# A third buffer for a block's scores and transpositions one slot later, in the attention stage of a decoder layer

## The reference, cut to what matters

```python
x = x + mamba_block(layernorm(x))                       # state-space block
x = x + cross_attention(ctx, ctx, layernorm(x), mask)   # 16 heads of 32, 750 keys
x = x + ffn(layernorm(x))                               # 512 -> 2048 -> 512, binarized weights
```

```python
qh = split_heads(q @ Wq + bq); kh = split_heads(k @ Wk + bk); vh = split_heads(v @ Wv + bv)
logits = einsum('bhqd,bhkd->bhqk', qh, kh) / sqrt(32) + mask * -1e9
attn = softmax(logits, axis=-1)
out = einsum('bhqk,bhkd->bhqd', attn, vh).merge_heads() @ Wo + bo
```

## Time and profile before

| | |
|---|---|
| median of three runs | 3586.39 us |
| the profiled execution | 3583.32 us, span 3582.0 us |
| PE busy over the span | 3233.6 us (90%) |
| DVE, ACT, POOL busy | 2664.0, 2390.2, 1804.9 us (74%, 67%, 50%) |
| exponentials, L1290 | 512 of 914 ns |
| mask and minimum, L1404 | 1024 of 544 ns |
| transpositions, L1163 | 3072 of 290 ns |
| copies of tiles 0 and 2, L1299 | 512 of 536 ns |

### The profile page before, as it was taken

The page is one execution under the profiler, slowest core; times in us unless marked ns, Lnnn a source line. Parts: engine busy times, 40 slices in busy tenths (PEclk is TensorE's granted clock), DMA queues, the critical chain, the costliest instruction groups (busy, mean ns, idle before and its releaser), DMA issues. The chain is left out here.

```text
span 3582.0 us, 59831 instructions
## 1 busy us (share of the span) xinstructions
PE 3233.6 (90%) x20864; PEld 2270.0 (63%) x20864; DVE 2664.0 (74%) x4673; ACT 2390.2 (67%) x5339; POOL 1804.9 (50%) x1211
## 2 busy tenths in 40 slices
PE   5699989898898988988997998999999999899999
PEld 4566655666566655666554666666666666678887
DVE  2899999999999999999984776667676676622222
ACT  5777888778877788777863667666666666622222
POOL 2678887888878888888873000000000000045454
PEclk8899999999999999999999999999999999999999
DMA  5576766667666766676564041111211121111010
GB/s 163 153 187 189 190 173 158 179 178 192 174 158 180 190 171 162 173 196 180 159 166 158 4 122 61 46 46 60 75 47 46 51 79 54 30 57 43 24 48 24
DMA packets 286282, 425.03 MB, mean 119 GB/s; under 512 B 28737, under 2 KB 226113, under 8 KB 281378
## 3 DMA queue, kind: packets, MB, share of 16 engines
q1 hardware_dynamic: 278621, 411.44, 41.1%
q10 hardware_dynamic: 7365, 9.77, 0.9%
HBM read 320.12 MB, written 101.02 MB: 118 GB/s over the span
## 5 line engine op out<-in xcount | busy, mean ns | idle before, releaser
L810 POOL TENSOR_TENSOR a_hs<-a_rep,a_bmat 128x896 f32<-128x896 f32 x512 | 1061.8, 2098 | 287.7 <-PE a_yps L322 286.3
L442 ACT ACTIVATE a_states<-a_rep,a_a_neg 128x224 f32<-128x224 f32 x2048 | 793.5, 437 | 90.2 <-DVE a_hs L706 88.2
L699 DVE TENSOR_TENSOR_SCAN a_states<-a_states,a_hs 128x900 f32<-128x900 f32 x384 | 779.8, 2031 | 75.6 <-ACT a_states L442 60.9
L1404 DVE CUSTOM_DVE_ANT_0 b_sc<-sps,early_mask 112x375 f32<-112x375 f32 x1024 | 499.8, 544 | 155.6 <-PE sps L1147 155.5
L1163 PEld LDWEIGHTS b_tps<-ident,b_sc 112*125 112x125 f32 x3072 | 404.1, 192 | 287.1 <-issue 167.9
L1163 PE MATMUL b_tps<-ident,b_sc 112*125 112x112 f32 x3072 | 493.6, 290 | 77.6 <-DVE b_pT L1418 36.4
L1290 ACT ACTIVATE b_sc<-b_sc,b_nmax 112x750 f32<-112x750 f32 x512 | 467.3, 914 | 62.9 <-DVE b_nmax L1410 62.7
L1546 POOL TENSOR_SCALAR b_x_var<-mv 112x2 f32<-112x2 f32 x16 | 3.4, 213 | 898.5 <-DVE mv L1455 898.5
L344 PE MATMUL a_work<-early_scan_hT,w_in 128*128 128x224 f32 x2048 | 425.6, 363 | 10.4 <-issue 7.5
L344 PEld LDWEIGHTS a_work<-early_scan_hT,w_in 128*128 128x128 f32 x2048 | 396.7, 196 | 51.5 <-issue 44.3
L706 DVE TENSOR_TENSOR a_hs<-a_states,a_cmat 128x896 f32<-128x896 f32 x384 | 419.0, 1091 | 13.2
(11 more groups left out here) (199 smaller groups left out, 5017.8 us busy)
## 6 DMA issues: line engine op xcount, KB each, us to landing
a_rep<-du_scratch SPq DMA_DIRECT2D x512, 224.0 KB, 5.7
w_in<-W_in_dram SPq DMA_DIRECT2D x128, 512.0 KB, 4.3
du_scratch<-early_du SPq DMA_DIRECT2D x16, 1792.0 KB, 11.6
ctx<-ctxT_dram SPq DMA_DIRECT2D x48, 500.0 KB, 5.9
v_scratch<-kv_out SPq DMA_DIRECT2D x96, 250.0 KB
k_scratch<-kv_out SPq DMA_DIRECT2D x96, 250.0 KB, 4.5
b_keys<-k_scratch SPq DMA_DIRECT2D x8, 1500.0 KB, 9.5
b_v<-v_scratch SPq DMA_DIRECT2D x8, 1500.0 KB
```

Of the source, the lines that this page charges most:

```text
L442: e = act.activation(rows(states[:, g % DA, :])[:, q, 1:ROW], rep[tile % REPS][:, j, 0, :], ACT.Exp, scale=a_neg[:, g % SLOTS, q:q + 1])
L699: dve.tensor_tensor_scan(state if g % G4 else whole, state, whole, 0.0, ALU.mult, ALU.add).then_inc(S["scan"], 1)
L810: pool.tensor_tensor(hs[g % RING][:, :, 1:ROW], rep[tile % REPS][:, j, 1, :].unsqueeze(1).broadcast_to([P, Q, L]), bmat[b % 2][:], ALU.mul ...
L1404: dve.tensor_tensor_reduce(out=sc[block % 2][:, j, cols], in0=sps[0:TT, j, 0:HALF], in1=mask[:, block % 2, cols], scale=-1.0, scalar=3.0e3 ...
```

## The change

Scores get a third buffer, `sc2`, which lies in the region `shared`. There it takes the place of the first half of w1, so this half is loaded near the end of the stage only: block n uses buffer n mod 3 up to block 122, and from block 123 on (`THREE`) two buffers in turn. The load of the first half of w1 waits for all transpositions of the first 123 blocks and stands at slot 249; its two signs stand in ACT's slots 254 and 255. The other half is loaded at slot 32 as before, with its two signs in slots 48 and 49. `nmax` has three places instead of two.

Transpositions and their copies move one slot later (`slot - 3`), for all tiles. Weighing the values, spreading the sums and keeping them (`rb`) move from slots 2, 6, 10, 14 to 3, 7, 11, 15, and `scale_o` from 3, 7, 11, 15 to 4, 8, 12, 0. Inverting the sums stays in slots 2, 6, 10, 14. The second output projection and its residual move from slot 7 to slot 6. At the end of the stage, the rows of the feed-forward part are normalised and transposed a little earlier.

```diff
         stats = mem.sbuf("stats", [TT, 2, 6])
-        sc = [mem.sbuf(f"sc{i}", [TT, GROUP, KEYS]) for i in range(2)]
+        sc = [*(mem.sbuf(f"sc{i}", [TT, GROUP, KEYS]) for i in range(2)),
+              mem.inside("sc2", [TT, GROUP, KEYS], shared.scores)]
         half_min = mem.sbuf("half_min", [TT, 2, GROUP])
-        nmax = mem.sbuf("nmax", [TT, 2, GROUP])
...
         LAST = (B - 1) * SLOTS
-        ROWS_AT = (LAST + 13, LAST + 15, LAST + 16, LAST + 17)
+        ROWS_AT = (LAST + 12, LAST + 13, LAST + 16, LAST + 17)
+        THREE = LAST // 2 + 3
+        assert THREE % 3 == 0 and (GROUP * KEYS <= 2 * F)
         tps = mem.psum("tps", [P, 2, BANK])
         ups = mem.psum("ups", [P, 2, BANK])
...
 
         slots = range(-6, B * SLOTS + SLOTS // 2 + 4)
         unit_of, bank_of = {}, {}
+
+        def buffer_of(block):
+
+            return block % 3 if block < THREE else (block - THREE) % 2
+
+        def used_by(block):
+
...
                 if 0 <= slot < N_ALL:
                     scores(slot)
                 if before:
-                    transpose_p(slot - 2, 0)
+                    transpose_p(slot - 3, 0)
                 for b in range(B):
                     at = slot - b * SLOTS
                     if -3 <= at < -3 + SLOTS and (at + 3) % 4 == 0:
                         project_q(b, (at + 3) // 4)
-                    if 6 <= at < 6 + SLOTS and (at - 6) % 4 == 0:
-                        weigh_v(b, (at - 6) // 4)
+                    if 7 <= at < 7 + SLOTS and (at - 7) % 4 == 0:
+                        weigh_v(b, (at - 7) // 4)
                 if before:
-                    transpose_p(slot - 2, 1)
+                    transpose_p(slot - 3, 1)
                 for b in range(B):
                     at = slot - b * SLOTS
                     if at == -4 and b:
                         transpose_h(b, 0)
                         transpose_h(b, 1)
-                    if 6 <= at < 6 + SLOTS and (at - 6) % 4 == 0:
-                        spread_sums(b * GROUPS + (at - 6) // 4)
+                    if 7 <= at < 7 + SLOTS and (at - 7) % 4 == 0:
+                        spread_sums(b * GROUPS + (at - 7) // 4)
                     if at == SLOTS + 4:
                         out_proj(b, 0)
-                    if at == SLOTS + 7:
+                    if at == SLOTS + 6:
                         out_proj(b, 1)
                 if before:
-                    transpose_p(slot - 2, 2)
+                    transpose_p(slot - 3, 2)
                 if slot in ROWS_AT:
                     transpose_rows(ROWS_AT.index(slot))
             for f in range(3):
...
-                act.activation(sc[block % 2][:, j, :], sc[block % 2][:, j, :], ACT.Exp, scale=-1.0,
-                               bias=nmax[:, block % 2, j:j + 1],
+                scores = sc[buffer_of(block)][:, j, :]
+                act.activation(scores, scores, ACT.Exp, scale=-1.0, bias=nmax[:, block % 3, j:j + 1],
                                accum_out=esum[:, block % 2, head:head + 1]).then_inc(S["exp"], 1)
 
...
 
-            def sign_w1(k):
-                act.wait_ge(S["w1_in"], 16)
+            def sign_w1(k, loaded):
+                act.wait_ge(S["w1_in"], 16 * loaded)
                 act.activation(shared.s1[:, k, :], shared.raw_1[:, k, :], ACT.Sign).then_inc(S["s1"], 1)
 
...
             for slot in slots:
-                before = 2 <= slot <= N_ALL + 1
-                if slot - 3 * SLOTS in range(KD):
-                    sign_w1(slot - 3 * SLOTS)
+                before = 3 <= slot <= N_ALL + 2
+                if slot - 3 * SLOTS in range(2):
+                    sign_w1(2 + slot - 3 * SLOTS, 1)
+                if slot - LAST - 14 in range(2):
+                    sign_w1(slot - LAST - 14, 2)
                 if slot - LAST - 10 in range(4):
                     sign_w2(slot - LAST - 10)
                 ready = 1 <= slot <= N_ALL
                 if before:
-                    keep_pT(slot - 2, 0)
+                    keep_pT(slot - 3, 0)
                 if ready and slot % 2 == 0:
                     exponential(2 * slot - 2)
                 for b in range(B):
...
                         keep_hT(b, 1)
-                    if 6 <= at < 6 + SLOTS and (at - 6) % 4 == 0:
-                        keep_sums(b * GROUPS + (at - 6) // 4)
+                    if 7 <= at < 7 + SLOTS and (at - 7) % 4 == 0:
+                        keep_sums(b * GROUPS + (at - 7) // 4)
                     if at == SLOTS + 9:
                         guess_rsqrt_x2(b)
                 if ready:
                     exponential(2 * slot - 1 - slot % 2)
                 if before:
-                    keep_pT(slot - 2, 2)
...
                     dve.wait_ge(S["nmax"], block)
-                if half == 0 and block >= 2:
-                    dve.wait_ge(S["t_ps"], 2 * PAIRS * (block - 1))
+                if half == 0 and block >= 3:
+                    dve.wait_ge(S["t_ps"], 2 * PAIRS * (used_by(block) + 1))
                 for j in range(GROUP):
                     dve.tensor_tensor_reduce(
...
                 for b in range(B):
                     at = slot - b * SLOTS
-                    if 7 <= at < 7 + SLOTS and (at - 7) % 4 == 0:
-                        scale_o(b, (at - 7) // 4)
+                    if 8 <= at < 8 + SLOTS and (at - 8) % 4 == 0:
+                        scale_o(b, (at - 8) // 4)
                 if 0 <= slot < N_ALL:
                     negate_and_mask(slot)
...
                 if before:
-                    keep_pT(slot - 2)
+                    keep_pT(slot - 3)
                 for b in range(B):
                     at = slot - b * SLOTS
                     if at == SLOTS + 4:
                         add_residual(b, 0)
-                    if at == SLOTS + 7:
+                    if at == SLOTS + 6:
                         add_residual(b, 1)
-                if slot == LAST + 11:
...
 
-            def load_w1():
-                sp.dma_start(shared.raw_1[:], t["w1T"].rearrange("(k p) f -> p k f", p=P)).then_inc(S["w1_in"], 16)
+            def load_w1(half):
+                if half == 0:
+                    sp.wait_ge(S["t_ps"], 2 * PAIRS * THREE)
+                sp.dma_start(shared.raw_1[:, 2 * half:2 * half + 2, :],
+                             t["w1T"].rearrange("(k p) f -> p k f", p=P)[:, 2 * half:2 * half + 2, :]
+                             ).then_inc(S["w1_in"], 16)
...
                 if slot == 2 * SLOTS:
-                    load_w1()
+                    load_w1(1)
+                if slot == LAST + 9:
+                    load_w1(0)
                 if slot == LAST - SLOTS:
```

More of the change, by code:

```diff
@@ L74, in __init__ @@
         self.beside_ctx = start + 4 * row - 96
+        self.scores = start
         self.raw_1, self.s1 = mem.inside("raw_w1", [P, D // P, F], start), mem.inside("s1", [P, D // P, F], start, F32R)
@@ L1074, in attention_phase @@
         unit_of, bank_of = {}, {}
+        def buffer_of(block):
+            return block % 3 if block < THREE else (block - THREE) % 2
+        def used_by(block):
+            return next((n for n in range(block - 1, -1, -1) if buffer_of(n) == buffer_of(block)), None)
         def loads(b):
@@ L1354, in scalar_program @@
                 if before:
-                    keep_pT(slot - 2, 2)
+                    keep_pT(slot - 3, 2)
                 if ready and slot % 2:
@@ L1400, in negate_and_mask @@
                     dve.wait_ge(S["nmax"], block)
-                if half == 0 and block >= 2:
-                    dve.wait_ge(S["t_ps"], 2 * PAIRS * (block - 1))
+                if half == 0 and block >= 3:
+                    dve.wait_ge(S["t_ps"], 2 * PAIRS * (used_by(block) + 1))
                 for j in range(GROUP):
                     dve.tensor_tensor_reduce(
-                        out=sc[block % 2][:, j, cols], in0=sps[0:TT, j, 0:HALF], in1=mask[:, block % 2, cols],
+                        out=sc[buffer_of(block)][:, j, cols], in0=sps[0:TT, j, 0:HALF], in1=mask[:, block % 2, cols],
                         scale=-1.0, scalar=3.0e38, op0=ALU.add, op1=ALU.min,
@@ L1409, in negate_and_mask @@
                     dve.wait_ge(S["ttr"], GROUP * (n + 1))
-                    dve.tensor_tensor(nmax[:, block % 2, :], half_min[:, 0, :], half_min[:, 1, :],
+                    dve.tensor_tensor(nmax[:, block % 3, :], half_min[:, 0, :], half_min[:, 1, :],
                                       ALU.min).then_inc(S["nmax"], 1)
@@ L1520, in vector_program @@
                         add_residual(b, 0)
-                    if at == SLOTS + 7:
+                    if at == SLOTS + 6:
                         add_residual(b, 1)
-                if slot == LAST + 11:
+                if slot == LAST + 10:
                     normalise_rows()
```

3 lines of the change are left out of this document (2 added, 1 removed).

## The result

| kernel | time, median (runs) | profiled span | mean granted clock |
|---|---|---|---|
| before | 3582.37 us (3576.38 to 3587.51, 4 runs) | 3582.0 us | 0.961 |
| changed | 3648.93 us (3645.95 to 3655.22, 4 runs) | 3645.2 us | 0.951 |

The ratio is 1.0189, interval 1.0164 to 1.0213: the change makes the kernel 1.9% slower. The forecast was 3617 us, slower, with a range of 3578 to 3652: the sign and the range hold, the range by 3 us (one of the four runs, 3655.22, lies above it). The forecast's own 3600 to 3640 does not hold it: half of the loss was not in the forecast's sum.

What follows compares the result with a forecast made beforehand. TensorE, 92% busy in the attention stage, was taken to set the pace, with its waits to gain or lose. The profiled 3583.32 us, +26 for batches, +7 for the end and nothing for the clock gave about 3617; range 3578 to 3652.

Steps and rivals of the forecast that it cites:

- Terms a to e: Changes in each attention batch's slots, summing to +1.75 us a batch, about fifteen times: +26 us.
- a: Slots 0 and 4: tiles come two ScalarE slots after their exponentials, so waits for these go: -1.7 us a batch.
- b: ScalarE's queue: copy of the sums stands ahead of both exponentials, lengthening slots 0, 4 and 10: +0.7 us a batch.
- d: Slot 10's statistics lose their covering weighing, so tile 0 of slot 11 waits for VectorE's copy: +1.4 us a batch.
- e: Slot 12: next batch's guess stands behind the sums' copy; tile 0 waits 2.4 us instead of 1.34: +1.05 a batch.
- c: Inverting the sums, no longer covered by the weighing, delays tile 0 of slots 3 and 15: +0.3 us a batch.
- Terms f to h: Stage's end: masks wait in slots 250, 252, 254, +5 us; signs of w1, +1.9 and -1.9; last weighing later, +2.
- The tail: After slot 255's scores: the last weighing's first exponential now starts behind the sums: +2 us.
- i: Late load of half of w1, about 16 us, first used over 20 us later: costs nothing, at most 16 us.
- the clock's term of the sum: Slow-clock stretches in attention batches stay at 1.8 us a batch: change 0, bounds -27 and +40 us.
- Much slower: the clock: Rival: new waits in slots 11 and 12 bring a slow-clock stretch in every batch, +40 us more, 3656 us; 15%.

Runs made afterwards that it cites:

- e4: Changed kernel with ScalarE's guess and first exponential ahead of the copy of the sums, and VectorE's tile 1 copy ahead of slot 10's statistics: 3534.51 us.
- e3: Changed kernel with the scores of slot 11 made twice and of slot 12 three times, in all batches but the last: 3595.67 us.
- e2: Changed kernel with VectorE's copy of tile 1 put ahead of slot 10's statistics for the next batch: 3597.45 us.
- e1: Changed kernel with ScalarE's guess for the next batch put ahead of its copy of the sums in slot 11: 3590.3 us.

## Why the prediction was right, and where its sum failed

**Terms a to e: right, in mechanism and size.** An undisturbed batch came out +1.52 us longer (72.85 against 71.33), forecast +1.75. Slots 0 and 4, where a and b meet, are together 1.17 us shorter (10.55 to 9.38), forecast -1.25, and the exponentials' waits are gone (a). The copy of the sums waits 3.1 us at a time, forecast 2.5; slots 0 and 10 last 3.43 and 3.42 instead of 3.07, and slot 4 0.20 more than in e4, which are b's three places (forecast 0.3, 0.3 and half of 0.3). e4's 0.9 is near b's 0.7 in part by chance: it has 0.3 from slot 12, which b did not name, and nothing from slot 10. Tile 0 of slot 11 comes 5.57 us after slot 10's scores, forecast 5.6, and mending it gives 1.17, forecast 1.4 (d); tile 0 of slot 12 waits 2.34, forecast 2.4 (e). Slots 10 to 12 take 15.55 us (3.42 + 6.65 + 5.48), forecast 15.5. What e was worth when mended, 2.07, is more than its +1.05, because the mend takes away the old wait of 1.34 as well. Slots 6 and 7 became 0.2 shorter together, where the forecast had nothing.

Term c was not tried alone, but the trace has it: slot 2 begins at 2491.76, VectorE's copy stands behind the inversion and starts 3.36 us later (forecast 3.35), and tile 0 of slot 3 comes 1.03 us after its scores, 0.2 behind the 0.83 that c took as possible. From copy to tile c writes 0.75; its own rows give 0.77, and nothing hangs on it. The first and the last row are TensorE's, the two between VectorE's:

```profile
2494.85 0.90 PE L1161 MATMUL sps<-b_keys,b_q 32*112 32x375 f32 x8
...
2494.84 0.36 DVE L1444 COPY b_rwide<-b_rsum 112x128 f32<-112x128 f32 x2
2495.12 0.62 DVE L1434 COPY b_pT<-b_tps 125x448 f32<-125x448 f32 x1
...
2495.88 0.66 PE L1177 MATMUL b_tps<-ident,b_sc 112*125 112x112 f32 x4
```

**Terms f to h: right in kind, too small.** +11.3 us against +7, and this with the first nine slots of the last batch 2.5 us shorter than before. Slots 250, 252 and 254 took 6.29, 6.30 and 7.61 us, forecast "near 5 us and more": scores there run at 1.61 us, the slow clock again. The tail is +5.0, forecast +2: what makes up the other 3 us was not tried. **Term i: right in that it costs nothing.** The two halves of w1 landed in 7.4 and 26.3 us, estimate 16 each; the late one is issued at 3137.64, 31 us ahead of its first sign (3168.66), so its first use did not wait for it.

**The step that failed is the clock's term of the sum: "I leave its 1.8 us as they are".** It was argued from the total of the waits, taken as 4.1 us a batch before and little more after. In the waits view the copies alone have 77.6 us after (43.5 + 34.1), where copies and exponentials together had 48.3 (26.7 + 3.2 + 18.4). Measured: the surplus over the undisturbed batch went from 22 to 57 us, +35, where the term had 0 with bounds of -27 and +40. The last rival, "Much slower: the clock", had the mechanism and 15%, and its 3656 is nearer to the 3649 than the forecast's 3617: all fourteen batches from 1 to 14 ran above 74 us, and e3 shows the slow clock to be the cause. So the wide range was right by reaching almost to this rival, not by the forecast's own sum. What spoke against the rival, an undisturbed batch that has a wait of 1.34 us and no slow stretch, showed only that such a wait need not bring one. With +35 for that term and +11 for the end, the same sum gives 3583 + 26 + 11 + 35 = 3655, against 3646.6 in the profiled execution; of the 9 us between them 4.8 lie ahead of the stage, and the rest is a to e, +22 instead of +26.

## What to carry to other kernels

When work is moved one slot along in several queues at once, read each queue for what now stands behind a waiting instruction: here two guesses of 0.20 us, one set of statistics and one copy decided between 1.9% slower and 1.3% faster (e4). A copy that frees a buffer for the bounding engine goes ahead of work that has a slot to spare. And a wait of TensorE can be priced twice, as idle time and as the slower clock that may follow it; where it can't be removed, filling it with repeated products is a test of that second price, and here gave it back.

## What was not expected of the hardware

The total of TensorE's waits did not tell the clock's price: VectorE's and ScalarE's copies cost 70.0 us of waits in 800 us in e2 (33.9 + 36.1) and 57.5 in e1 (21.9 + 35.6), yet in the profiled executions the surplus is 16 us in e2 and 28 in e1. In that execution of e2 the slow stretches stop after batch 4 while every batch keeps the same wait of slot 12. And e2, one kernel, took from 3592.12 to 3621.32 us, in the main the longer the lower its mean granted clock (0.963 to 0.955), so the stretches need not come alike in each execution. Why these four batches and not the later ones, and why this kernel spreads more than the others, stays open: no run here tells it.
